# Graph network on one core: the attention layer's normalized features put back into their convolution place while its last chunk is still being finished

## The reference, cut to what matters

```python
h = x @ W                                   # layer 0
e = s_src[row] + s_dst[col]; e = where(e > 0, e, 0.2 * e)
att = softmax of e over each row's edges
x1 = x + elu(segment_sum(att[:, None] * h[col], row))
for l in range(3):                          # layer 1, starts from xh1 = relu(norm(x1))
    agg = segment_sum((xh @ W[l])[src] * norm[:, None], dst) + b[l]
    xh = layer_norm(relu(agg)) + xh
```

## Time and profile before

| | |
|---|---|
| median of 3 runs | 2400.73 us (2398.84 to 2401.29) |
| the profiled execution | 2394.39 us, of it 2392.5 us span |
| TensorE busy | 2180.5 us, 91% of the span |
| VectorE / ScalarE / GpSimd busy | 1035.9 / 770.7 / 630.3 us |
| mean granted TensorE clock | 0.949 |
| first instruction of the attention's last tail after the steps (L1046) | 659.91 us |
| first DMA of `convolutions` | 672.53 us |
| first convolution matmul | 680.48 us |
| first matmul of `recurrent` | 957.46 us |

### The profile page before, as it was taken

How to read it: one execution, slowest core, us unless ns; L and a number is a source line. 1 busy time by engine, 2 the same in 40 slices (tenths; PEclk the granted TensorE clock), 3 DMA queues, 4 the chain that set the end, 5 groups by cost and what they waited for, 6 DMA issues and landing times.

```text
span 2392.5 us, 27783 instructions
## 1 busy us (share of the span) xinstructions
PE 2180.5 (91%) x9986; PEld 1202.6 (50%) x9987; DVE 1035.9 (43%) x2906; ACT 770.7 (32%) x1403; POOL 630.3 (26%) x432
## 2 busy tenths in 40 slices
PE   5799788998869995998999999999999999998998
PEld 3344387555525553454445554565445544554444
DVE  7799889999835456232121211212121111213202
ACT  3577577887723233221111111111111110112200
POOL 3000000000024432433444344433444344440000
PEclk8899955999989997999999999999999999999999
DMA  6200091444421122333122322223222322135582
GB/s 183 67 8 8 12 303 40 132 158 144 139 46 1 1 36 72 63 65 89 22 35 44 75 33 44 34 47 76 26 34 42 74 33 31 22 62 186 208 308 95
DMA packets 185817, 185.51 MB, mean 78 GB/s; under 512 B 110530, under 2 KB 172705, under 8 KB 181740
## 3 DMA queue, kind: packets, MB, share of 16 engines
q1 hardware_dynamic: 119658, 136.95, 18.1%
q0 software_dynamic: 56752, 1.28, 7.0%
q10 hardware_dynamic: 9281, 45.63, 5.2%
HBM read 100.45 MB, written 83.36 MB: 77 GB/s over the span
## 4 chain that ended last, share of the span: by engine, by line
PE 55%; DMA 3%; DVE 1%; issue 0%; ACT 0%; DVEq 0%; ACTq 0%
PE banks L1691 25%; PE banks L1716 21%; PE banks L1813 6%; DMA feat<-hnD 3%; PE banks L1769 1%; PE banks L1677 1%; DMA out_dram<-big 0%; PE banks L1778 0%; PE banks L1831 0%; DVE HN L1984 0%; DVE banks L1979 0%; ACT banks L1876 0%; DVE HN L1981 0%; PE banks L1794 0%; DVE big L2028 0%
## 5 line engine op out<-in xcount | busy, mean ns | idle before, releaser
L882 POOL DMA_INDIRECT WT<-lists x391 | 607.4, 1553 | 856.2 <-DMA WT<-lists 842.3
L1691 PE MATMUL banks<-big,feat 125*128 125x500 f16 (+1 forms) x3150 | 605.7, 353 | 20.7 <-DMA feat<-hnD 16.5
L1691 PEld LDWEIGHTS banks<-big,feat 125*128 125x128 f16 x3150 | 306.2, 97 | 310.4 <-DMA feat<-hnD 17.2
L1716 PE MATMUL banks<-H,U 128*128 128x500 f32 (+1 forms) x756 | 302.7, 541 | 8.0 <-issue 7.9
L1716 PE MATMUL banks<-aT,V 128*128 128x500 f32 (+1 forms) x756 | 296.4, 538 | 3.0 <-DVE HN L1984 3.0
L1716 PEld LDWEIGHTS banks<-aT,V 128*128 128x128 f32 x756 | 143.1, 190 | 145.1 <-issue 97.4
L1716 PEld LDWEIGHTS banks<-H,U 128*128 128x128 f32 x756 | 142.6, 191 | 137.6 <-issue 100.2
L1972 DVE SCALAR_TENSOR_TENSOR HN<-banks,bh,HN 128x500 f32<-128x500 f32 (+1 forms) x70 | 47.8, 682 | 375.8 <-ACT HN L1874 353.6
L1874 ACT ACTIVATE HN<-banks,bs 128x500 f32<-128x500 f32 (+1 forms) x70 | 44.3, 632 | 379.9 <-PE banks L1716 379.9
L1097 PE MATMUL banks<-work 125*128 125x500 f32 (+1 forms) x350 | 158.3, 566 | 5.3 <-DMA work<-xhD 3.1
L1334 PE MATMUL banks<-big,G 125*128 125x500 f16 (+1 forms) x700 | 141.5, 359 | 23.2 <-DVE G L1424 23.2
(11 more groups left out here) (294 smaller groups left out, 2339.5 us busy)
## 6 DMA issues: line engine op xcount, KB each, us to landing
big<-WT ACTq DMA_DIRECT2D x25, 1562.5 KB, 7.7
WT<-zero SPq DMA_DIRECT2D x39, 980.0 KB, 9.5
hTD<-HN SPq DMA_DIRECT2D x40, 250.0 KB, 2.1
hnD<-stg SPq DMA_DIRECT2D x32, 250.0 KB
feat<-hnD SPq DMA_DIRECT2D x4, 2000.0 KB
H<-hTD SPq DMA_DIRECT2D x16, 500.0 KB, 4.8
work<-xhD SPq DMA_DIRECT2D x28, 250.0 KB
WT<-lists POOLq DMA_INDIRECT x391, 3.0
```

Source lines behind the costliest of these rows:

```text
L882: nc.gpsimd.indirect_dma_start(out=WT, out_offset=bass.IndirectOffsetOnAxis(ap=lists[:, 0, t - first:t - first + 1], axis=0), in_=lists[:, ...
L1691: last = nc.tensor.matmul(SUMS[s % 2][half][:, 0:wid(ch)], rows_, A[:, j, cols(ch)], start=(j == 0 and part == 0), stop=(j == T - 1 and pa ...
L1716: last = nc.tensor.matmul(PS[bank][:, 0:w], wt_[:, kt, g:g + 128], v[:, kt, 0:w], start=(n == 0), stop=(n == len(terms) - 1))
```

## The change

One permanent allocation, `room` (128 partitions x 2 x 3200 f32), takes the place of `trow`, `ecol`, `wp` and `feat`. Its first half holds `trow` until the attention's last logit and is called `early` from then on: it is the same memory as `xr` of the convolutions. Its second half holds `ecol` and `wp`, then some of the attention's small buffers (`half`, `PT`, `hT` with `e_` over it, and the weights), then `x2`. The attention's remaining buffers are one allocation `work`.

In the attention's SP program, after the 49 steps and ahead of the last chunk's x1D store, SP waits for the last logit and then issues three loads of xh1D into `early`: tiles 0 to 7, 8 to 15 and 16 to 21, each once the stores of its chunks have landed. The last chunk (tiles 22 to 24) is not stored to xh1D any more: ScalarE's clip writes it straight into `early`. The three loads at the start of `convolutions` are gone; ScalarE and VectorE wait there for the four new semaphores instead.

```diff
+        landed = [sem("early_" + n) for n in ("a", "b", "c", "d")]
+        room = kept("room", [128, 2, T * D])
+        trow = room[0:P + 1, 0, 0:N]
...
+            ecol = room[:, 1, 0:4 * EG * LANE].rearrange("p (i e) -> p i e", i=4)
...
+        feat = room[0:P].rearrange("p h n -> p (h n)").bitcast(f16).rearrange("p (t a d) -> p t a d", a=2, d=S2)
...
+GROUPS = ((0, 0, 2 * NQ), (1, 2 * NQ, 4 * NQ), (2, 4 * NQ, FIRST[SC - 1]))
...
+        ZB, XB, TB, HB = 2 * NQ * CH, RX * NQ * D, RP * CH, NQ * D
+        work = sb("work", [P, ZB + XB + 2 * HB])
...
+        early = room[0:P, 0, :].rearrange("p (t d) -> p t d", d=D)
+        spare = room[:, 1, :]
...
@@ attention, SP
+                sp.wait_ge(l_r, len(unit_list))
+                for s_, lo, hi in GROUPS:
+                    sp.wait_ge(xh_out, 16 * (CHUNK[hi - 1] + 1))
+                    sp.dma_start(early[:, lo:hi, :], xh1D[:, lo:hi, :]).then_inc(landed[s_], 16)
                 stores(SC - 1)
-                normed(SC - 1)
                 sp.wait_ge(x1_out, 16 * SC)
-                sp.wait_ge(xh_out, 16 * SC)
                 sp.wait_ge(zeros, 16 * ZF)
@@ attention, ScalarE
-                    nc.scalar.activation(y[:, 0:rows[ch], :], y[:, 0:rows[ch], :], ACT.Relu).then_inc(xh_r, 1)
+                    end = ch == SC - 1
+                    to = early[:, FIRST[ch]:T, :] if end else y[:, 0:rows[ch], :]
+                    nc.scalar.activation(to, y[:, 0:rows[ch], :], ACT.Relu).then_inc(landed[3] if end else xh_r, 1)
@@ convolutions, SP
-                for s_, lo, hi in groups:
-                    sp.dma_start(xr[:, lo:hi], xh1D[:, lo:hi]).then_inc(s_, 16)
@@ convolutions, ScalarE (VectorE alike)
-                    for s_, lo, hi in groups:
+                    for s_, lo, hi in GROUPS:
                         if lo == ch * NQ:
-                            act.wait_ge(s_, 16)
+                            act.wait_ge(landed[s_], 16)
+                    if ch == FIRST[SC - 1] // NQ:
+                        act.wait_ge(landed[3], 1)
```

More of the change, by code:

```diff
@@ new lines, in gnn_kernel, with sb @@
+        trow = room[0:P + 1, 0, 0:N]
+        with ExitStack() as c:
+            def sb(name, shape, dt=f32):
+                return c.enter_context(nc.sbuf_tensor(name, shape, dt))
+            ecol = room[:, 1, 0:4 * EG * LANE].rearrange("p (i e) -> p i e", i=4)
+            edges = dict(
+                ecol=ecol,
+                comb=ecol[:, 0],
+                sib=ecol[:, 1],
+                keyc=ecol[:, 2],
+                wc=ecol[:, 3],
+                wp=room[:, 1, 4 * EG * LANE:6 * EG * LANE].bitcast(bf16).rearrange("p (e i) -> p e i", i=4),
+                rank=sb("rank", [128, 1], i32),
+                wcol=sb("wcol", [128, 2, SB * LANE]),
+                visits=sb("visits", [1, 4, 160], i32),
+                pairs=sb("pairs", [128, WC], f16),
+                nodes=sb("nodes", [128, P], f16),
+                first=sb("first", [128, NW]),
+                place=sb("place", [128, EG * LANE]),
+                past=sb("past", [128, NW]),
+                dump=sb("dump", [128, 1]),
+                rows=sb("rows", [8, RD, BATCH, 2, LANE], f16),
+                scol=col[:, 0, :],
+                trow=trow,
+                ident=ident,
+                identh=identh)
+            prepare(nc, sem, PS, big, edges, x, src, dst, ew, aW, aA, gW, wih, whh, l0w, l1w, w1, w2,
+                    digD, nearD, VD, whhD, l0D, l1D, w12D, xhD)
+            counts(nc, sem, PS, banks, A, edges, sD, digD, scatD, WT)
@@ new lines, in gnn_kernel @@
+        attention(nc, sem, PS, x, aW, xhD, x1D, xh1D, A, trow[0:P], ident, identh, col, scat_sems, scatD, WT,
+                  room, landed)
+        feat = room[0:P].rearrange("p h n -> p (h n)").bitcast(f16).rearrange("p (t a d) -> p t a d", a=2, d=S2)
+        convolutions(nc, sem, PS, cW, cB, scat_sems, scatD, WT, x1D, x2D, hTD, xhTD, A, ident, identh, col, feat, landed)
+        recurrent(nc, sem, PS, bih, bhh, l0b, l1b, b1, b2, out, scat_sems, scatD, WT, VD, whhD, l0D, l1D, w12D, x2D, xhTD, hnD, hTD,
+                  big, A, ident, feat)
@@ L885, in scatter, with attention @@
         pool.wait_ge(added, 16 * (t + 1))
-def attention(nc, sem, PS, x, aW, xhD, x1D, xh1D, A, trow, ident, identh, col, scat_sems, scatD, WT):
+GROUPS = ((0, 0, 2 * NQ), (1, 2 * NQ, 4 * NQ), (2, 4 * NQ, FIRST[SC - 1]))
+def attention(nc, sem, PS, x, aW, xhD, x1D, xh1D, A, trow, ident, identh, col, scat_sems, scatD, WT, room, landed):
     with ExitStack() as c:
@@ L893, in attention @@
         zero = sb("zero0", [128, 1, ZN])
[L895 to L904, removed]
+        ZB, XB, TB, HB = 2 * NQ * CH, RX * NQ * D, RP * CH, NQ * D
+        work = sb("work", [P, ZB + XB + 2 * HB])
+        z = work[:, 0:ZB].rearrange("p (u n) -> p u n", n=CH)
+        xh = work[:, ZB:ZB + XB].rearrange("p (r k d) -> p r k d", r=RX, d=D)
+        y, t = (work[:, ZB + XB + i * HB:ZB + XB + (i + 1) * HB].rearrange("p (k d) -> p k d", d=D) for i in range(2))
+        junk = work[:, N:2 * N]
+        early = room[0:P, 0, :].rearrange("p (t d) -> p t d", d=D)
+        spare = room[:, 1, :]
+        half = spare[0:P, 0:2 * CH].rearrange("p (h n) -> p h n", h=2)
+        PT = spare[0:P, 2 * CH:2 * CH + TB].rearrange("p (r n) -> p r n", r=RP)
+        both = spare[:, 2 * CH + TB:2 * CH + TB + HB]
+        hT, e_ = both[:, 0:CH], both[0:P].rearrange("p (k d) -> p k d", d=D)
+        W = spare[:, 2 * CH + TB + HB:2 * CH + TB + HB + D]
         mx = sb("mx", [P, 4, T])
@@ L912, in attention @@
         oneh = sb("oneh", [P, 1], f16)
-        neg = z[:].rearrange("p u n -> p (u n)").bitcast(f16)[:, 0:2 * N].rearrange("p (h n) -> p h n", h=2)
+        neg = work[:, 0:N].bitcast(f16).rearrange("p (h n) -> p h n", h=2)
         names = ("made", "loaded", "neg_r", "mx_r", "deg_r", "al_r", "l_r", "e_r", "p_r", "tp_r", "ev_r",
@@ L1230, in _, with convolutions @@
                 center(SC - 1)
-def convolutions(nc, sem, PS, cW, cB, scat_sems, scatD, WT, xh1D, x1D, x2D, hTD, xhTD, A, ident, identh, col, feat):
+def convolutions(nc, sem, PS, cW, cB, scat_sems, scatD, WT, x1D, x2D, hTD, xhTD, A, ident, identh, col, feat, landed):
     with ExitStack() as c:
@@ L1256, in convolutions @@
         st = sb("st1", [P, 2, 4, NQ])
-        names = ("loaded", "xa", "xb", "xc", "hi_r", "g_r", "agg_r", "aT_r", "o_r", "y_r", "rl_r", "var_r", "nb_r", "n_r",
+        names = ("loaded", "hi_r", "g_r", "agg_r", "aT_r", "o_r", "y_r", "rl_r", "var_r", "nb_r", "n_r",
                  "x_r", "chain", "x1_in", "x2_out", "pair_r", "tr_r", "hs_r", "hs_out0", "hs_out1")
-        (loaded, xa, xb, xc, hi_r, g_r, agg_r, aT_r, o_r, y_r, rl_r, var_r, nb_r, n_r,
+        (loaded, hi_r, g_r, agg_r, aT_r, o_r, y_r, rl_r, var_r, nb_r, n_r,
          x_r, chain, x1_in, x2_out, pair_r, tr_r, hs_r, hs_out0, hs_out1) = (sem("c_" + i) for i in names)
         hs_out = (hs_out0, hs_out1)
-        x_in = (xa, xb, xb, xc, xc, xc, xc)
-        groups = ((xa, 0, NQ), (xb, NQ, 3 * NQ), (xc, 3 * NQ, T))
-        assert CL == 3 and SC == len(x_in)
+        assert CL == 3
         S, B0 = CL * SC, (CL - 1) * SC
@@ L1477, in _ @@
                     dve.wait_ge(hi_r, ch * NQ + rows[ch])
-                    for s_, lo, hi in groups:
+                    for s_, lo, hi in GROUPS:
                         if lo == ch * NQ:
-                            dve.wait_ge(s_, 16)
+                            dve.wait_ge(landed[s_], 16)
+                    if ch == FIRST[SC - 1] // NQ:
+                        dve.wait_ge(landed[3], 1)
                     for q in range(rows[ch]):
```

## The result

The changed kernel takes 2393.30 us in the median of 22 runs (2390.14 to 2396.90), the kernel before 2398.97 us in 22 runs (2393.93 to 2403.53): 5.7 us faster, ratio 0.9976 with a 95% interval of 0.9969 to 0.9982. The profiled execution has a span of 2390.3 us against 2392.5.

The account below looks back on a forecast made before the run. TensorE's matmuls were taken to bound the kernel, with stops waiting for split features. An earlier start (4.0 us) and shorter first sum (5.5) gave 2400.7 - 9.5 = 2391.2 us, range 2389 to 2395, chance 0.68; 8 in 10: 2386.5 to 2397.0.

Parts of the forecast that it names:

- what takes the removed wait's place: End of attention: the removed store's 3.0 us wait brings nothing by itself, since the x1D store behind the early loads replaces it.
- a store that is not held up: Rival at the attention's end: x1D store passes the loads, Block starts at 669.5, 13.0 us gained, 2387.7 us; chance 0.14.
- the crawling loads: Rival in the attention's tail: early loads move at 50 GB/s, Block starts at 691.1, 8.6 us slower, 2409.3 us; chance 0.05.
- One sign: In SP's chain at the attention's end: the three early loads would be issued by 658.
- the term "1.9": Attention's end: time the x1D store needs after the early loads, 1.5 to 1.9 us, taken as 1.9.
- 670.3 + 1.9 + 0.8 = 673.0: Convolutions' Block start: early loads' end, x1D store, then last data to Block; bounds 671.6 and 673.9.
- 4.0 us gained: Start of the convolutions: TensorE's first matmul at 676.5 instead of 680.48.
- From the Block's start to the first matmul: Start of the convolutions: 1.0 us to ScalarE's first split, then 2.5 us to TensorE's first matmul.
- the first sum: TensorE in the convolutions: 10.57 + 0.45 + 1.7 (slow start) = 12.7 us against 18.17, no stops; 5.5 us gained, bounds 3.8 to 5.7.
- the case of a low clock throughout: Rival in the convolutions' first sum: TensorE's clock stays low, 22.0 us, nothing changes, 2400.5 us; chance 0.05.
- something given back: Rival: recurrent stage's transfers or a held-up x load take back gain, leaving 3 to 5 us, 2396.7 us; chance 0.08.
- my own test: Second sum's first matmul to span's end stays 1693.8 us; growth above 2 us would mean gain was given back there.

Follow-up runs that it names:

- f1: The changed kernel with two early loads (tiles 0 to 15), the third issued at the start of the convolutions; 10.2 us faster than before, ratio 0.9957.
- f4: The changed kernel with one more 125-row transfer of 0.38 MB, read by nobody, behind the three early loads; ratio 0.9982 against before.
- e3: The changed kernel with each early load and the last x1D store cut into rows 0 to 111 and 112 to 124; ratio 0.9948 against before.
- e5: The kernel before, with only its three xh1D loads at the convolutions' start cut into rows 0 to 111 and 112 to 124; ratio 0.9983.
- e1: The changed kernel with the last chunk's x1D store issued by ScalarE on its own DMA queue; ratio 0.9973 against before.
- e2: The kernel before with the last chunk clipped into place and not stored, other tiles loaded at the convolutions' start in regrouped loads; ratio 0.9980.
- f2: The changed kernel with early loads and last x1D store split in rows, plus the hnD reloads and output stores split alike; 2370.31 us, ratio 0.9879.
- f3: The kernel before with the last chunk clipped into place, no early loads, and the convolutions' three loads split in rows; ratio 0.9965.

## Why the prediction was right, and where it was off

**Right: what takes the removed wait's place.** The x1D store behind the early loads delays the Block, and the Block starts later after the clip than before, not earlier. f1 and f4 show that bytes on five engines do it, e3 that more engines end it. The case of a store that is not held up is out, and so are the crawling loads: the rate was 113 to 133 GB/s from 660 to 672. One sign came out otherwise: the third load was issued at 659.9 and not by 658, since SP waited 2.4 us for the store before it, which had been issued at 655.16. It cost nothing that the windows show, because earlier loads kept the queue busy.

**Mis-sized: the time that the x1D store takes.** It was the term "1.9" in "670.3 + 1.9 + 0.8 = 673.0". With the tail 0.72 us late the forecast is 673.7, and the Block started at 676.24, 2.5 us later and 1.6 beyond the bound. The windows and packet sizes put nearly all of that at one term. The store's first packets come at about 671.5, where the loads' end was put at 670.3 + 0.7 = 671.0: 0.5 us, inside the bound. From there the store needs 3.9 us and not 1.9: it shares its first two microseconds with the last packets of the loads, and then a part of it drains at 25 GB/s on what the share says is one engine. From its last packet to the Block it is 0.8 us, as predicted. In f1 the store's packets take 3.8 us as well (673.2 to 677.0) and the Block again starts 0.9 us behind them, so this excess does not depend on the bytes ahead. What makes one engine end late stays open. So TensorE's start gained 1.4 us against the clip (10.25 for 11.66) where "4.0 us gained" was predicted.

**Right: from the Block's start to the first matmul.** 1.04 us to the first split, 2.51 to the first matmul; 1.0 and 2.5 were predicted. Both stops of TensorE are gone.

**Slightly too short: the first sum.** It took 13.2 us and not 12.7; the slow start cost 2.2 us where 1.7 was taken, inside the bounds. 5.0 us gained for 5.5. The first-sum lengths of the other kernels with unbroken feed are 12.8 to 13.6 us, so this term moves by that much from one execution to the next. The clock rose once here (0.50 until 684, 0.93 from 684 to 686, then 1.00); the case of a low clock throughout is out.

**The sum.** 1.4 + 5.0 = 6.4 us at the seam for 9.5. The medians say 5.7, which is below the 6.9 to 10.6 us that the bounds gave. That the time itself, 2393.30 us, lies only 2.1 us from the forecast of 2391.2 and inside its bounds is in part luck: the forecast started from 2400.73 us, the median of three runs, and 22 runs of the same kernel gave 2398.97. This hides 1.8 us of the 3.8 that are missing. One bound is also added up wrongly: a start at 671.6 gains 5.4 us and not 4.9, so the upper end is 11.1 us.

**Was something given back?** By my own test it was: the distance from the second sum to the end of the span is 1697.3 us against 1693.8. But in e5, which has nothing of the change, it is 1695.0, in the others that keep the stage after it 1696.6 to 1700.7, a spread of 4.1 us among kernels with the same code there; and the execution of before that was profiled is 4.6 us under the median of the 22, the profiled one after only 1.2 us under. The distance scatters by more than the 2 us that I had set as the mark. The medians decide: in all eight kernels that leave the stage after it alone, the gain in the medians matches that at the marks within 0.8 us. By them nothing was given back that can be measured; the traces alone do not show it.

## What to carry to other kernels

Before loads are issued early, ask which transfer must still land before the next barrier, and count the bytes that will be ahead of it on the same DMA engines; the part of the loads that delays it costs more than it brings (two early loads beat three by 3.1 us at the marks). Look at a transfer's share of the DMA engines first: here it was a third, and cutting 125 rows into 112 and 13 on top of the change was worth 7.6 us where the change had gained 5.7. Alone, in the kernel before, it was worth 4.6, and in two places that the prediction did not look at, 17.6 more. Judge a local change at local marks in several traces, since one whole execution scatters by more than such a change is worth.

## What the runs showed of the hardware

- The 125-row transfers of this seam use 0.31 to 0.36 of the 16 DMA engines and move 128 to 133 GB/s at most, with one load or three outstanding; as 112 and 13 rows the same bytes use all (share 0.97 and more) and reach 300 GB/s.
- The engines do not end together: behind 1.4 MB of loads the last 1.6 us of a 0.19 MB store ran at 25 GB/s and a share of 0.07 or less, with the same in f1. Alone on the engines in the kernel before, a store of this size moved all its packets in 2.2 us.
- Two queues on the same engines get equal turns by packet and not by byte: 55 packets with 0.08 MB beside 57 with 0.18 MB in the same 2 us (e1). The second queue with small packets got the smaller share and did not overtake. The Trainium skill, "DMA: Bandwidth & Descriptors", "Queues, rings and completion order", says that each engine goes round its queues packet by packet. The near-equal counts agree with that, and the unequal bytes follow from them; the page's packet holds several descriptors, and no run here shows how many of the profile's packets go before a switch.
- The meeting of all engines between Blocks costs 0.26 to 0.28 us after the last engine's work when no transfer is awaited (e2, e3, f2, f3).
